# Gated cross-attention and grouped mixture of experts on one core: the order of work in the fill

## What is computed

```
xa  = x + tanh(g_xattn) * attention(layernorm(x), ctx, ctx)      # causal, Wq, Wk, Wv, Wo, bo
z   = layernorm(xa), cut into groups of 32 rows
lg  = z @ controller + ramp;  perm = (lg == max over the group)
y   = relu(perm' z @ f1 + bias) @ f2, put back to rows by perm
out = xa + tanh(g_ffn) * y
```

## Time and profile before

| what | us |
|---|---|
| median of 3 runs | 309.36 |
| lowest and highest | 309.05, 312.26 |
| the profiled execution | 311.98 |
| its span, first to last instruction | 310.3 |

### The profile page before, as it was taken

How to read it: one execution, slowest core, us unless ns; L and a number is a source line. 1 busy time by engine, 2 the same in 40 slices (tenths; PEclk the granted TensorE clock), 3 DMA queues, 4 the chain that set the end, 5 groups by cost and what they waited for, 6 DMA issues and landing times.

```text
span 310.3 us, 8572 instructions
## 1 busy us (share of the span) xinstructions
PE 243.7 (79%) x3426; PEld 193.9 (62%) x3426; DVE 197.7 (64%) x433; ACT 168.3 (54%) x345; POOL 124.1 (40%) x230
## 2 busy tenths in 40 slices
PE   0617163798989899898888878698998888789995
PEld 0617052776768687686666656476766777677773
DVE  4574755496859779485777799989995443412222
ACT  1521243485877768485757645336785443334553
POOL 4140233557776767675556665624541000000000
PEclk9985765599999999799989999979999999859999
DMA  6929985647677675738551000049940000001211
GB/s 175 212 92 185 288 167 100 142 109 163 149 178 139 150 162 133 162 65 182 116 138 23 4 4 5 0 145 396 388 161 2 3 4 4 4 2 68 69 68 68
DMA packets 21961, 35.87 MB, mean 116 GB/s; under 512 B 2915, under 2 KB 15779, under 8 KB 20387
## 3 DMA queue, kind: packets, MB, share of 16 engines
q1 hardware_dynamic: 21059, 34.01, 43.1%
q10 hardware_dynamic: 864, 1.33, 1.9%
HBM read 26.65 MB, written 8.39 MB: 113 GB/s over the span
## 4 chain that ended last, share of the span: by engine, by line
PE 27%; POOL 24%; issue 23%; DVE 13%; DMA 7%; ACT 4%; SPq 1%; POOLq 0%; DVEq 0%
POOL pT L377 9%; PE banks L763 7%; PE banks L735 6%; DMA cT<-in_ctxT_dram 6%; PE banks L472 4%; PE banks L772 3%; POOL xs L371 3%; POOL qp L362 3%; POOL kp L362 2%; DVE permb L1144 2%; POOL onl L401 2%; DVE rsum L1099 2%; DVE gmax L1130 1%; PE banks L581 1%; DVE lt L1125 1%
## 5 line engine op out<-in xcount | busy, mean ns | idle before, releaser
L1091 DVE TENSOR_REDUCE nmax<-banks 128x4 f32<-128x512 f32 x64 | 43.7, 685 | 37.5 <-PE banks L535 37.5
L377 POOL TENSOR_SCALAR_AFFINE_SELECT pT<-pT 128x512 f32<-128x512 f32 x64 | 40.7, 637 | 45.4 <-ACT pT L866 45.3
L866 ACT ACTIVATE pT<-banks 128x512 f32<-128x512 f32 x64 | 37.6, 590 | 8.2 <-PE banks L552 7.8
L871 ACT ACTIVATE banks<-cb 128x512 f32<-128x512 bf16 x62 | 37.0, 596 | 5.6 <-DVE nmax L1091 5.5
L581 PE MATMUL banks<-pT,va 128*32 128x128 f32 x512 | 27.7, 289 | 0.8 <-POOL pT L377 0.8
L535 PE MATMUL banks<-kst,qst 96*128 96x128 bf16 x256 | 26.7, 231 | 1.7 <-ACT banks L871 1.4
L1099 DVE RECIPROCAL rsum<-banks 128x256 f32<-128x256 f32 x16 | 28.0, 1748 | 0.0
L552 PE MATMUL banks<-qst,kst 99*128 99x128 bf16 x256 | 25.9, 225 | 1.0 <-ACT pT L866 1.0
L581 PE MATMUL banks<-pT,ones 128*32 128x128 f32 x512 | 26.4, 279 | 0.0
L763 PEld LDWEIGHTS banks<-cf,routed 128*128 128x128 f32 x128 | 21.1, 250 | 7.2 <-issue 6.2
L985 ACT ACTIVATE ys<-banks 128x1024 f32<-128x1024 f32 x16 | 16.7, 1046 | 16.0 <-PE banks L763 16.0
(11 more groups left out here) (115 smaller groups left out, 633.4 us busy)
## 6 DMA issues: line engine op xcount, KB each, us to landing
wx<-in_wexp_dram SPq DMA_DIRECT2D x32, 256.5 KB, 6.8
q_rows<-qp SPq DMA_DIRECT2D x8, 384.0 KB, 2.5
k_rows<-kp SPq DMA_DIRECT2D x8, 384.0 KB, 4.9
qst<-q_rows SPq DMA_DIRECT2D x8, 384.0 KB, 4.7
kst<-k_rows SPq DMA_DIRECT2D x8, 384.0 KB, 4.8
cT<-in_ctxT_dram SPq DMA_DIRECT2D x8, 256.0 KB, 6.7
qst<-q_rows SPq DMA_DIRECT2D x8, 256.0 KB, 5.5
kst<-k_rows SPq DMA_DIRECT2D x8, 256.0 KB, 5.6
```

The costliest lines, as they stand in the source:

```text
L377: pool.affine_select(p, p, [[0, HC], [1, P]], ALU.is_ge, 0.0, base=0, channel_multiplier=-1)\
L866: act.activation(pT[:, n % PR, :], BT[n % 2], ACT.Exp, scale=float(D) ** -0.5).then_inc(p_ready, 1)
L871: act.activation(BS[n % 2], causal, ACT.Copy).then_inc(mask_placed, 1)
L1091: dve.tensor_reduce(nmax[:, b % 2, :].rearrange("p (e j o) -> p e o j", e=2, o=KH)[:, e, o], BS[n % 2].rearrange("p (j t) -> p j t", j=HC) ...
```

## The change

The fill is put in another order on all engines but PE, whose instructions stay as they are but for one wait.

- Transfers: ScalarE issues the identity part of the constants alone (64 KB, semaphore `ident_loaded`), then K and Q. The rest of the constants, V, WO and the gates go to SP's queue. SP loads x for batches 0 to 3 and contexts 0 and 1 first, then context 2 (which waits for `c_ready` 1), V, batches 4 to 7, the shift rows; K is kept and stacked ahead of Q. The loads of batches 8 to 15 are cut in two (`XL`) and stand, with WO, the rest of the constants and the controller, behind the stacks of pair 1.
- VectorE: one statistics chain for batches 0 to 3, not two for two each; `weight_low(K)` leaves; it takes the low part of Q of pair 0 (`q_low_first`).
- GpSimd: takes K's low part of the weight (`weight_low_by_dim`, four instructions of 128x128), contexts 0 to 2 before K's low part of pair 0; the controller's copy moves to slot 56, `weight_low(WO)` to slot 4.
- ScalarE: `weight_high(K)` first, `context_high(1)` and `(2)` and `weight_high(V)` earlier, K's parts before Q's, `weight_high(WO)` in slot 3.

```diff
-XL = ((0, 2), (2, 4), (4, 8), (8, 16))
+XL = ((0, 2), (2, 4), (4, 8), (8, 12), (12, 16))
             load_x(0)
+            load_x(1)
             load_context(0)
+            load_context(1)
+            load_context(2)
+            sp.dma_start(w[:, V], wattn[:, V]).then_inc(w_loaded[V], 16)
+            load_x(2)
             sp.wait_ge(shift_ready, 1)
             sp.dma_start(kst[SROWS:TROWS]...
-            load_x(1)
-            load_context(1)
-            load_x(2)
+            keep_k(0)
             keep_q(0)
-            keep_k(0)
+            stack_k(0)
             stack_q(0)
-            stack_k(0)
+            sp.dma_start(gb[:, :], gbo).then_inc(gates_loaded, 16)
+            load_context(3)
+            keep_k(1)
+            keep_q(1)
+            stack_k(1)
+            stack_q(1)
             load_x(3)
-            load_context(2)
-            keep_q(1)
-            keep_k(1)
-            stack_q(1)
-            stack_k(1)
-            load_context(3)
+            sp.dma_start(w[:, WO], wattn[:, WO]).then_inc(w_loaded[WO], 16)
+            load_x(4)
+            sp.dma_start(cf[:, P:], constf[:, P:]).then_inc(consts_loaded, 16)
             sp.dma_start(ctrl_in[:, :, :], ctrl).then_inc(small_loaded, 16)
...
+            def weight_low_by_dim(m):
+                pool.wait_ge(w_high, 1)
+                for j in range(2 * KH):
+                    out, high = [t[:, m].rearrange("p k (o d h) -> p (k o) d h", o=KH, d=D)[:, j] for t in (wl, wh)]
+                    last = pool.tensor_tensor(out, w[:, m].rearrange("p k (o h d) -> p (k o) d h", o=KH, d=D)[:, j],
+                                              high.bitcast(F32), ALU.subtract)
+                last.then_inc(w_low[m], 1)
...
-            pool.wait_ge(consts_loaded, 16)
+            pool.wait_ge(ident_loaded, 16)
             pool.tensor_copy(identb, ident).then_inc(masks_ready, 1)
-            context_low(0)
-            low_part(qp, 2, qr, 1, 0, qm_ready, ql_ready)
+            weight_low_by_dim(K)
+            for g in range(3):
+                context_low(g)
             low_part(kp, 0, kr, 1, 0, km_ready, kl_ready)
-            context_low(1)
+            weight_low(V)
+            low_part(kp, 0, kr, 1, 1, km_ready, kl_ready)
             low_part(qp, 2, qr, 1, 1, qm_ready, ql_ready)
-            low_part(kp, 0, kr, 1, 1, km_ready, kl_ready)
-            context_low(2)
-            weight_low(V)
-            pool.wait_ge(small_loaded, 16)
-            pool.tensor_copy(ctrl_sb...
-            weight_low(WO)
...
+                if n == 4:
+                    weight_low(WO)
...
+                if n == CH - 8:
+                    pool.wait_ge(small_loaded, 16)
+                    pool.tensor_copy(ctrl_sb...
...
-            pe.wait_ge(consts_loaded, 16)
+            pe.wait_ge(ident_loaded, 16)
...
-            act.dma_start(cf[:, :], constf).then_inc(consts_loaded, 16)
-            for i in range(2):
+            act.dma_start(ident, constf[:, 0:P]).then_inc(ident_loaded, 16)
+            for i in (K, Q):
                 act.dma_start(w[:, i], wattn[:, i]).then_inc(w_loaded[i], 16)
...
-            for i in range(2, 4):
-                act.dma_start(w[:, i], wattn[:, i]).then_inc(w_loaded[i], 16)
-            act.dma_start(gb[:, :], gbo).then_inc(gates_loaded, 16)
...
+            weight_high(K)
             context_high(0)
-            weight_high(K)
             weight_high(Q)
             xT_high(0, BB)
+            context_high(1)
             k_high(0)
+            k_mid(0)
             q_high(0, bank[4])
             q_mid(0)
-            k_mid(0)
-            context_high(1)
+            context_high(2)
+            weight_high(V)
             xT_high(1, bank[3])
             k_high(1, bank[5])
+            k_mid(1)
             q_high(1, bank[2])
             q_mid(1)
-            k_mid(1)
-            context_high(2)
-            weight_high(V)
...
-            weight_high(WO)
...
+                if n == 3:
+                    weight_high(WO)
...
+            def q_low_first():
+                dve.wait_ge(qm_ready, 1)
+                dve.tensor_tensor(qp[:, 2, :], qr[:, :], qp[:, 1, :], ALU.subtract).then_inc(ql_ready, 1)
...
-            rstd_rows(0, 2)
+            rstd_rows(0, 4)
             normalize_x(0)
             normalize_x(1)
-            weight_low(K)
             weight_low(Q)
             xT_low(0, BB)
+            normalize_x(2)
+            normalize_x(3)
             k_rest(0)
             q_rest(0, bank[4])
-            rstd_rows(2, 4)
-            normalize_x(2)
-            normalize_x(3)
+            q_low_first()
             xT_low(1, bank[3])
...
+                    dve.wait_ge(consts_loaded, 16)
```

More of the change, by code:

```diff
@@ L147, in build @@
         x_loaded = [sem(f"x_loaded{i}") for i in range(len(XL))]
+        ident_loaded = sem("ident_loaded")
         consts_loaded = sem("consts_loaded")
@@ L412, in keep_perm @@
                 pool.tensor_copy(permT[:, b, :], pc[:, k, :]).then_inc(permT_kept, 1)
-            pool.wait_ge(consts_loaded, 16)
+            pool.wait_ge(ident_loaded, 16)
             pool.tensor_copy(identb, ident).then_inc(masks_ready, 1)
-            context_low(0)
-            low_part(qp, 2, qr, 1, 0, qm_ready, ql_ready)
+            weight_low_by_dim(K)
+            for g in range(3):
+                context_low(g)
             low_part(kp, 0, kr, 1, 0, km_ready, kl_ready)
-            context_low(1)
+            weight_low(V)
+            low_part(kp, 0, kr, 1, 1, km_ready, kl_ready)
             low_part(qp, 2, qr, 1, 1, qm_ready, ql_ready)
-            low_part(kp, 0, kr, 1, 1, km_ready, kl_ready)
-            context_low(2)
-            weight_low(V)
-            pool.wait_ge(small_loaded, 16)
-            pool.tensor_copy(ctrl_sb[:, :, :].rearrange("p h (s e) -> p h s e", s=NS),
-                             ctrl_in[:, :, :].rearrange("p h (e s) -> p h s e", s=NS)).then_inc(ctrl_ready, 1)
-            weight_low(WO)
             for n in range(SLOTS_N):
@@ L443, in _ @@
                     bias_x(n // 4)
+                if n == CH - 8:
+                    pool.wait_ge(small_loaded, 16)
+                    pool.tensor_copy(ctrl_sb[:, :, :].rearrange("p h (s e) -> p h s e", s=NS),
+                                     ctrl_in[:, :, :].rearrange("p h (e s) -> p h s e", s=NS)).then_inc(ctrl_ready, 1)
                 if s == 5 and g + 3 < NG2:
```

## The result

| what | before | changed |
|---|---|---|
| median of 20 runs, us | 311.38 | 313.02 |
| lowest and highest | 306.66, 316.88 | 311.24, 314.49 |
| profiled span | 310.3 | 312.0 |

The ratio of changed to before is 1.011, with a 95% interval of 1.008 to 1.014. The change makes the kernel about 1% slower. The forecast was 308.2 us, or 1.1 us less than before; the measured change is in the other direction, and the time lies above the range's 311.5. The median of before over 20 runs lies 2 us above that of the 3 runs known then, so sizes are compared as differences. (A ratio leaves out runs over 1.5% above the fastest of their kernel; a median here is over all runs, so the two can differ a little.)

The account below looks back on a forecast made before the run. It took everything ahead of slot 8 (61.42 us) as fill made by three waits. Slot 8 2.4 us earlier, less 1.3 lost to PE's half clock, gave -1.1 us: from 309.36 to 308.2 us, range 303.0 to 311.5.

Parts of the forecast that it names:

- the controller's wait: Fill, GpSimd: its 9.91 us wait for the controller's load, until 51.39, delays the split PE awaits until 56.09; it goes.
- The start of x: Kernel start: second x load lands at 8.3, the normalization chain ends at 14.0, first rows leave at 25.7 against 20.27.
- The late loads as the next bound: SP's queue behind pair 1's stacks: x lands at 54.4, VectorE's statistics wait, slot 8 starts about 59.0, 2.4 us earlier.
- the queue ahead of `place_max(0)`: SP's queue before slot 8: late loads and pair 2's K rows stand ahead of `place_max(0)`, which comes at 58.6.
- First scores: Pair 0's rows to `spread_max(0)`: first scores at 39.7, `spread_max(0)` at 48.5 not 56.09, WO's parts costing nothing.
- the exclusion of GpSimd and VectorE: First statistics chain: GpSimd's SBUF-reading subtractions hold up VectorE's two-input instructions, adding about 1.3 us.
- The term for the clock: Slots 8 to 11: after idling, PE runs some 3 us at half clock, losing 1.3 us (bounds 0 and 2.4).
- 7.6 us gained at `spread_max(0)`: Before slot 8: `spread_max(0)` starts at 48.5, not 56.09; by PE's own work slot 8 would follow at 53.8.
- the early queue: Rival: stacks or first rows come 2 to 4 us sooner, slot 8 gains 6.4 to 7.6, about 303.5 us; chance 0.33.
- The slower one: Rival: second x load lands near 14.0, first rows issued at 31, slot 8 at 64.7, 314 us; chance 0.10.
- Nothing moves: Rival: queue, 2 us longer, replaces the controller's wait; slot 8 at 61, within 0.5 us of 309.4; chance 0.07, small loss included.
- The late start: Pair 0: the first rows leave at 25.7 instead of 20.27, 5.4 us later.

Follow-up runs that it names:

- e3: Changed kernel with both WO weight parts in slot 7 and VectorE's statistics of batches 8 to 15 four slots later; median 311.3 us, ratio to before 1.000.
- e2: Changed kernel with both WO weight parts (ScalarE's high, GpSimd's low) in slot 7 instead of slots 3 and 4; median 310.8 us, ratio to before 1.008.
- e1: Kernel before with only GpSimd's controller copy moved to slot 56 and its weight_low(WO) to slot 7; median 303.5 us, ratio to before 0.977.
- e9: Changed kernel with the start of x undone (context 0 ahead of second x load, two statistics chains); median 310.4 us, ratio to before 0.984.
- e7: Changed kernel with the five late loads just behind the shift rows and the start of x undone; median 305.1 us, ratio to before 0.984.
- e8: Kernel before with e1's edit, plus context 2 and x of batches 8 to 15 issued ahead of pair 0's rows; median 304.6 us, ratio to before 0.973.
- e4: Changed kernel with only the five late loads moved in SP's queue to just behind the shift rows; median 307.0 us, ratio to before 0.988.
- e5: As e4, with GpSimd's context_low(2) behind K's low part of pair 0 instead of ahead of it; median 306.5 us, ratio to before 0.988.

## Why the prediction was wrong

**Right.** The reading that the controller's wait held slot 8. The start of x: second x load landed at 8.4 (8.3 forecast), first rows out at 26.27 (25.7). The forecast of 39.7 is that of the mask's matmul, so 40.1 for the first scores themselves: 41.2 in the profile of the changed kernel, 39.2 to 41.2 over the runs with that start. Context 2's wait gone, `project_k(2)` where it was. The maxima ready and split at 49.7 (48.5). The late loads as the next bound: x at 55.5 (54.4), and the queue ahead of `place_max(0)`: e3 has slot 8 at 59.15, released by it, for 58.6 forecast (though not behind the K rows of pair 2, as the sum had it). With ScalarE's wait taken out the structure is the one that was priced: e2 has slot 8 18.9 us behind the first scores, for 18.9 forecast (59.0 - 40.1).

**The step that failed** is in *First scores*: "WO's parts and the controller's copy cost nothing: GpSimd waits in slots 4 and 56 anyway". It looked at the engine for GpSimd's part alone. WO's load had moved from ScalarE's queue, where it landed before 14, to SP's, behind the stacks and half of the late x, and `weight_high(WO)` on ScalarE, in slot 3, ahead of the masks, was costed at nothing. The same page of the working priced the x load in the same place for VectorE, one load ahead of WO. WO landed at 56.2, ScalarE stood 7.64 us, and `spread_max(0)` came at 57.9 instead of 48.5. As VectorE and the queue would have waited nearly as long, only 2.6 us of the 7.6 reach slot 8, by the profiles of the changed kernel and e2. With it the sum would have been -1.1 + 2.6 = +1.5 us; the medians say +1.6, the spans +1.7.

**Terms of another size.** Slot 8 was forecast at 59.0 and came at 62.6, 3.6 us later: 2.5 lie between first scores and slot 8, where ScalarE's wait is, and 1.1 were there at the first scores. Of these, 0.7 is the exclusion of GpSimd and VectorE on the statistics chain, put at 1.3 and measured at 2.0: each of K's four small weight subtractions, which I counted as hidden but for the last, holds one VectorE operation (0.38 to 0.48 us instead of 0.16).

The term for the clock, 1.3 us lost behind slot 8, had no counterpart in the profile. It priced some 3 us of half clock behind a slot 8 at 59. PE worked without a gap from 57.37 and, by the length of its matmuls, came to full clock at about 61.7 (about 61.5 before); as slot 8 came at 62.6, the half-clock time lay ahead of it, and the clock from 60 to 70 us is 0.91 against 0.92 before. In e2, with slot 8 at 58.0, PE was at half clock until about 61.5, as the term had it. So the forecast put slot 8 1.1 us too early at its first scores and took back 1.3 for the clock: that the corrected sum, +1.5, meets the measured +1.6 is in part luck.

**A gain that was sized wrongly.** The prediction has 7.6 us gained at `spread_max(0)`, from 56.09 to the 48.5 at which its operand is ready. But PE had waited only 5.63 us there, so by its own work it comes at 50.5, and at most 5.6 us can be gained; slot 8 by PE's own work alone would then be at 55.8, not 53.8. In e1 that part is the 5.6 above; the 7.1 at slot 8 and 7.6 by the medians lie near the forecast for other reasons. The 2.4 us of the sum come from the queue and do not use it, but the price of the early queue, 303.5, does. Two smaller slips: 8.3 + 7.5 should be 8.3 + 7.3 by the chain that is cited, and the 345 KB per us stands in no row that is shown.

**The rivals.** The slower one ended on the right side for a wrong reason: it asked for the second x load near 14, and that load came at 8.4. "Nothing moves" was nearest in time, but it asked for 2 us more of queue, and it was an engine's wait that came. The early queue did not come about, as forecast. The late start, 5.4 us at the first rows in the prediction, is worth 4.7 us there, 5.1 at the first scores and 3.2 at slot 8 (e9) if the queue is free, and nothing that shows if it is full (e7).

## What to carry to other kernels

When a load is moved down a queue, list every instruction on every engine that waits for it, not only the one that the load was moved for; what is queued behind that instruction, here the mask for `scores(5)` and those after it behind a weight that is first used in slot 19, is what it can cost. A transfer that is not urgent can go into a gap of the queue, and the gap has a size: 1.3 MB fitted here (e8), while 1.5 MB behind another 1.1 MB kept the rows in the queue for 6.4 us instead of 2.6 (e7) and hid everything upstream. And an isolated edit, tried first, would have shown that one of the many parts (taking away a 9.9 us wait on GpSimd) carries all the gain that these runs can tell. What a wait is worth is read at the engine that is held in the end: 9.91 us on GpSimd, but 5.63 on PE.

## What the runs showed of the hardware

**Stacks are slow transfers.** The stacks, reads into 48, 32 and 16 partitions with 8 KB each, move 1.5 MB in 11.0 us from first issue to last landing, or 140 KB per us, where x and context over 128 partitions move 320. The Trainium skill (SBUF — State Buffer, Door 1: The DMA port swizzle) says that partitions 0 to 63, where the read of 48 lies, reach only half of the 16 ports, and it gives 196 GB/s for these 64 and 104 for partitions 0 to 15. The trace, with all three sizes together, lies between the two; that the ports are the cause is not shown by a run here.

**SP's own issue can block.** In e4, e5 and e7 the issue of WO's load took 4 us of SP's time (3.98 in the row above), where it takes 0.50 in the changed kernel. In e4, 1.4 MB had been issued and not landed when it began (V, two loads of x, the shift rows), and it ended at 18.26, as the first of these two x loads landed (18.1). The bytes alone do not explain it: in the changed kernel the same late loads were issued right behind 1.5 MB of stacks, in 0.43 to 0.50 us each. What limit it met, no run here shows.

**The clock makes equal programs unequal.** From 40 us on e4 and e5 run the same instructions on PE, with first scores 0.4 us apart. Busy time by stretch, e4 and then e5 (the third figure from the end is the granted clock):

```profile
40.00:50.00 10.00, 7.24 (x59) 6.31 (x59) 7.42 (x15) 6.66 (x13) 5.07 (x9) 0.89 0.97 196
```

```profile
40.00:50.00 10.00, 7.67 (x43) 6.72 (x41) 6.03 (x12) 5.99 (x11) 3.60 (x7) 0.50 0.95 197
```

At a mean of 0.89 PE makes 59 matmuls in these 10 us, at 0.50 (1.2 GHz throughout) 43, and slot 8 follows the first scores by 13.4 us in the one and 15.9 in the other. In e5 PE has no wait from 48.65 to slot 8, so the 2.5 us are its own work at the lower clock, as much as ScalarE's wait cost. It is also why a single profile's slot 8 and span (e4: 301.3) should be read beside the median (307.0). What sets which level a run gets at that point is left open.
